# A fused attention and mixture-of-experts block: a shorter gate, own orders for the first and last steps, and the third norm and the logits moved

## The reference

```python
q, k = sigmoid(x @ Wq + bq), sigmoid(x @ Wk + bk);  v = x @ Wv + bv      # 16 heads of 8
sink_in = n / sum(q * cumsum(k));      src_out = n / sum(k * cumsum(q))
cons_sink = sum(q * cumsum(k * src_out)) / n;  cons_src = clip(sum(k * cumsum(q * sink_in)) / n, -1, 1)
v = v * exp(cons_src) / cumsum(exp(cons_src)) * n;   kv = cumsum(k x v)   # outer products, 8x8 a head
h = LN(x + (q * sink_in/n @ kv * sigmoid(cons_sink)) @ Wo + bo)           # first norm
x2 = LN(x + LN(h + gelu(h @ W1 + b1) @ W2 + b2))                          # second and third norm
scores = softmax(x2 @ gate_w + gate_b); top 2 of 8 experts, gate = sum of the two scores
out = LN(x2 + gate * sum over the 2 experts of relu(x2 @ wi + bi + lora_e(x2)) @ wo + bo)   # fourth
```

## Time and profile before

| | |
|---|---|
| median of 3 runs | 451.16 us (450.88 to 452.06) |
| the profiled execution, its own time | 451.44 us |
| its span, first to last instruction | 449.6 us |
| mean granted clock of PE | 0.907 of full |
| busy share PE, DVE, POOL, ACT | 85%, 76%, 50%, 46% |

### The profile page before, as it was taken

The page is one execution under the profiler, slowest core; times in us unless marked ns, Lnnn a source line. Parts: engine busy times, 40 slices in busy tenths (PEclk is TensorE's granted clock), DMA queues, the critical chain, the costliest instruction groups (busy, mean ns, idle before and its releaser), DMA issues.

```text
span 449.6 us, 6354 instructions
## 1 busy us (share of the span) xinstructions
PE 383.4 (85%) x2052; PEld 277.0 (62%) x2052; DVE 341.6 (76%) x819; ACT 208.2 (46%) x375; POOL 226.0 (50%) x263
## 2 busy tenths in 40 slices
PE   4675688488998998899989999899989997897792
PEld 1454556385647873696558665777478756664542
DVE  2448965998799789979897979978997899723522
ACT  2220064247543575446663674167435743554321
POOL 1013633863486349731993359426863498442201
PEclk9556969598999899899998999989998999997897
DMA  8108002700260018000730045002700170000000
GB/s 269 76 7 204 1 0 57 178 2 1 60 176 0 1 27 215 17 1 1 169 89 1 1 111 147 1 1 54 205 1 1 29 183 1 1 24 1 0 23 23
DMA packets 19856, 26.56 MB, mean 59 GB/s; under 512 B 1648, under 2 KB 9968, under 8 KB 19824
## 3 DMA queue, kind: packets, MB, share of 16 engines
q1 hardware_dynamic: 19680, 25.96, 22.6%
q10 hardware_dynamic: 144, 0.21, 0.2%
HBM read 7.29 MB, written 2.10 MB: 21 GB/s over the span
## 4 chain that ended last, share of the span: by engine, by line
PE 38%; DVE 24%; POOL 12%; issue 11%; DMA 7%; ACT 4%; SPq 3%; POOLq 0%; DVEq 0%; ACTq 0%
POOL prod L686 7%; PE pB L332 6%; PE pY L478 5%; DVE kv L870 4%; DMA vb<-vs 4%; PE pY L413 4%; PE pO L386 4%; PE pG L403 4%; DMA xT<-x_t 3%; DVE cum_kv L876 3%; SPq L274 3%; PE pA L320 2%; DVE cum_ks L766 2%; PE pG L467 2%; POOL rstd L676 2%
## 5 line engine op out<-in xcount | busy, mean ns | idle before, releaser
L686 POOL TENSOR_TENSOR prod<-cum_kv,q_fac 128x512 f32<-128x512 f32 x64 | 93.6, 1468 | 24.0 <-DVE cum_kv L876 17.0
L386 PEld LDWEIGHTS pO<-s_wor,prod 128*128 128x128 f32 x512 | 65.8, 200 | 31.7 <-POOL prod L686 22.8
L386 PE MATMUL pO<-s_wor,prod 128*128 128x128 f32 x512 | 70.8, 288 | 15.3 <-POOL prod L686 15.1
L870 DVE TENSOR_TENSOR kv<-k,vb 128x512 f32<-128x512 f32 x64 | 55.3, 864 | 5.5 <-DMA vb<-vs 5.4
L673 POOL TENSOR_TENSOR var_eps<-mv,s_con 128x4 f32<-128x4 f32 x32 | 11.4, 357 | 91.9 <-DVE mv L890 91.9
L876 DVE TENSOR_TENSOR_SCAN cum_kv<-p_ones,cum_kv,kv 128x512 f32<-128x512 f32 x32 | 40.5, 1274 | 0.6
L636 ACT ACTIVATE relu<-pG,s_att 128x512 f32<-128x512 f32 x32 | 21.9, 686 | 38.2 <-PE pG L460 38.0
L478 PEld LDWEIGHTS pY<-s_moe,gel 128*128 128x128 f32 x256 | 36.5, 223 | 4.7 <-issue 4.7
L876 DVE TENSOR_TENSOR_SCAN cum_kv<-p_ones,kv 128x512 f32<-128x512 f32 x32 | 38.5, 1214 | 0.5
L968 DVE SCALAR_TENSOR_TENSOR gel<-pG,neg_bi,relu 128x512 f32<-128x512 f32 x32 | 23.2, 743 | 19.0 <-PE pG L467 19.0
L478 PE MATMUL pY<-s_moe,gel 128*128 128x128 f32 x256 | 37.1, 305 | 0.0
(11 more groups left out here) (135 smaller groups left out, 776.6 us busy)
## 6 DMA issues: line engine op xcount, KB each, us to landing
vb<-vs SPq DMA_DIRECT2D x64, 256.0 KB, 4.6
xT<-x_t SPq DMA_DIRECT2D x8, 256.0 KB, 4.9
xt<-x SPq DMA_DIRECT2D x8, 256.0 KB, 5.3
out<-y SPq DMA_DIRECT2D x8, 256.0 KB, 2.3
s_moe<-moe_w SPq DMA_DIRECT2D x1, 836.0 KB, 10.3
s_wor<-wo_rep SPq DMA_DIRECT2D x1, 512.0 KB, 8.2
s_ffn<-ffn_w SPq DMA_DIRECT2D x1, 512.0 KB, 8.8
s_con<-consts SPq DMA_DIRECT2D x1, 502.0 KB, 5.0
```

The lines of the kernel that those rows point to most:

```text
L386: mm = pe.matmul(pO3[:, s, :], prod[:, m % 4, s * P:(s + 1) * P], s_wor[:, m, :], start=False, stop=(m == DH - 1), skip_group_check=True)
L686: pool.tensor_tensor(prod[:, m % 4, :], cum_kv[t.par][:, m, :], q_fac[t.par][:, :], ALU.mult).then_inc(prod_ready, 1)
L870: dve.tensor_tensor(kv[:, m % 3, :], k[t.par][:, :], vb[:, m, :], ALU.mult).then_inc(kv_ready, 1)
```

## The change

Five edits. (1) The gate has 13 DVE steps instead of 18: the maxima are searched in the logits less their maximum and in their exponentials, not in the normalised scores; the sum of exponentials and its inverse (`sum_exp`, `inverse_sum_exp`) leave the numbered chain, and `gate_total` is `(top2 + 1) * r_ex`. (2) PE, ACT, DVE (and POOL for its second step) get hand-written `opening`, `second_step` and `closing`; steps 1 to 7 still come from `step`, and SP's order is untouched. In the opening PE gets 14 matmuls without use (`keep_busy`), v of tile 0 gets a bank of its own, and ACT runs one sigmoid of one column before the weights are there. In the closing the last tile uses four banks instead of two. (3) In `step`, `moments(c,2)` stands behind the last `outer_product` of the next step, and POOL's `inverse_std(c,2)` behind `product(b,6)`. (4) `x2_T`, `logits` and with them the gate's first steps go behind the first head sums; `expert_out(d,0)` and `(d,1)` go ahead of them. (5) `gate_exp` goes behind `normalise(b,0)` on ACT.

```diff
-GATE_STEPS = 18
+GATE_STEPS = 13
 # PE
+            def opening(a):
+                project_q(a); project_k(a); project_v(a)
+                keep_busy(2)
+                head_sums(a, 0, True); head_sums(a, 0, False)
+                keep_busy(2)
+                denominators_T(a, 0); denominators_T(a, 1)
+                keep_busy(3)
+                head_sums(a, 1, True); head_sums(a, 1, False)
+                keep_busy(1)
+                cumulate_e(a)
+                keep_busy(2)
+                compensation_T(a); factor_T(a)
+                constant_row()
+                project_q(a.plus(1)); project_k(a.plus(1))
+                keep_busy(4)
+                reduce_out(a, 0)
+            def second_step(b):
+                for m in range(1, 5):
+                    reduce_out(b, m)
+                head_sums(a, 0, True); head_sums(a, 0, False); project_v(a)
+                reduce_out(b, 5)
+                denominators_T(a, 0); denominators_T(a, 1)
+                reduce_out(b, 6)
+                head_sums(a, 1, True); head_sums(a, 1, False)
+                reduce_out(b, 7)
+                cumulate_e(a); h_T(b); compensation_T(a); factor_T(a)
+                (hidden, ffn_out, reduce_out(a, 0))
+            def closing(c):
+                inter_base(d, 2); inter1(d, 2); expert_out(d, 0); inter_base(d, 3); inter1(d, 3); expert_out(d, 1)
+                inter2(d, 2); inter2(d, 3); expert_out(d, 2); expert_out(d, 3)
+                x2_T(c); logits(c)
+                inter_base(c, 2); inter_base(c, 3)
+                lora_in(c)
+                inter_base(c, 0); inter_base(c, 1)
+                u_T(c, True); u_T(c, False)
+                (inter1 x4, inter2(0), inter2(1), expert_out and inter2 in turn)
             def step(s):
-                if B: reduce_out(b, 2)
-                if C: x2_T(c)
-                if B: reduce_out(b, 3); reduce_out(b, 4)
-                if C: logits(c)
-                if B: reduce_out(b, 5); reduce_out(b, 6); reduce_out(b, 7)
-                if D: expert_out(d, 0)
+                if B: reduce_out(b, 2); reduce_out(b, 3); reduce_out(b, 4)
+                if D: expert_out(d, 0)
+                if B: reduce_out(b, 5); reduce_out(b, 6); reduce_out(b, 7)
+                if D: expert_out(d, 1)
                 if A: head_sums(a, 0, True); head_sums(a, 0, False); project_v(a)
+                if C: x2_T(c)
+                if D: expert_out(d, 2)
+                if A: denominators_T(a, 0)
+                if C: logits(c)
+                if A: denominators_T(a, 1)
 # ACT
+            act.activation(table_probe[:, :], onesrow[:, 0:1], ACT.Sigmoid)
-                if C: normalise(c, 2); x2T_out(c); gate_exp(c)
-                if A: v_out(a); spread_denominators(a, 0)
+                if C: normalise(c, 2)
+                if A: v_out(a)
+                if C: x2T_out(c)
+                if A: spread_denominators(a, 0); spread_denominators(a, 1)
                 if B: normalise(b, 0)
-                if A: spread_denominators(a, 1)
+                if C: gate_exp(c)
 # POOL
-                if B: product(b, 1); product(b, 2)
+                if B: product(b, 1); product(b, 2); product(b, 3); product(b, 4); product(b, 5); product(b, 6)
                 if C: inverse_std(c, 2)
-                if B: product(b, 3); product(b, 4); product(b, 5); product(b, 6); product(b, 7); inverse_std(b, 0)
+                if B: product(b, 7); inverse_std(b, 0)
 # DVE
                 if B: cumulate_kv(b, 5); outer_product(b, 6); cumulate_kv(b, 6); outer_product(b, 7)
+                if C: moments(c, 2)
                 if B: cumulate_kv(b, 7)
-                if A: cumulate_q(a); cumulate_k(a)
+                if A: cumulate_q(a); cumulate_k(a); k_times_cum_q(a, 0)
                 if D: second_relu(d, 2); second_relu(d, 3)
-                if A: k_times_cum_q(a, 0)
-                if C: gate(c, 0)
                 if A: q_times_cum_k(a, 0)
-                if C: gate(c, 1)
                 if B: moments(b, 0)
-                if C: gate(c, 2)
-                if A: inverse_denominators(a)
-                if C: gate(c, 3)
-                if A: normal_denominators(a)
-                if C: gate(c, 4); gate(c, 5)
-                if C: gate(c, 6); gate(c, 7)
+                if A: inverse_denominators(a); normal_denominators(a)
+                if C: gate(c, 0); gate(c, 1); gate(c, 2); gate(c, 3)
                 if A: sink(a)
                 (from here on one gate call between two calls of tile a, fewer ahead of expert_residual)
-                if B: moments(b, 2)
```

More of the change, by code:

```diff
@@ L56, in wait, with run_steps @@
     eng.wait_ge(sem, value)
-def run_steps(step):
-    for n in range(-1, TILES + 2):
+def run_steps(step, first=-1, end=TILES + 2):
+    for n in range(first, end):
         step(Tile(n))
@@ L534, in step @@
                 if A: factor_T(a)
-                if C: inter1(c, 0); inter1(c, 1); inter2(c, 0); inter2(c, 1)
+                if C: inter_base(c, 0); inter1(c, 0); inter_base(c, 1); inter1(c, 1); inter2(c, 0); inter2(c, 1)
                 if A: reduce_out(a, 0)
-            run_steps(step)
+            opening(Tile(0))
+            second_step(Tile(0))
+            run_steps(step, first=1, end=TILES)
+            closing(Tile(TILES - 1))
         @block.scalar
@@ L740, in _, with second_step @@
             pool.wait_ge(con_loaded, 16)
+            def second_step(b):
+                a = b.plus(1)
+                for m in range(1, DH):
+                    product(b, m)
+                inverse_std(b, 0); e_normal(a); scaled_h(b); h_residual(b); attention_input(a)
+                shifted_x(b); inverse_std(b, 1); product(a, 0); scaled_n2(b)
             def step(s):
@@ L757, in step @@
                 if B: scaled_n2(b)
-            run_steps(step)
+            step(Tile(-1))
+            second_step(Tile(0))
+            run_steps(step, first=1)
         @block.vector
@@ L1020, in step @@
[L1020 to L1021 removed]
                 if A: conserved(a)
[L1023 removed]
+                if C: gate(c, 11)
                 if A: clip_source(a)
@@ L1026, in step @@
                 if A: prefix_e(a)
-                if C: gate(c, 16)
+                if C: gate(c, 12)
                 if A: allocation(a)
-                if C: gate(c, 17); gate_total(c); masked_lora(c, False)
+                if C: gate_total(c); masked_lora(c, False)
                 if A: inverse_cum_e(a); source_factor(a); sink_factor(a)
```

219 lines of the change are left out of this document (155 added, 64 removed).

## The result

The changed kernel takes 459.16 us (median of 4 runs, 456.92 to 462.18) against 451.16: 1.018 times as long, with an interval of 1.012 to 1.024. The forecast was 437 us, faster, with a range of 429 to 446; it is slower, and outside the range. The profiled execution took 457.09 us, with a span of 455.2 us. The four times go with the mean clock granted to PE: 456.92 and 457.09 at 0.917 and 0.914, 461.23 and 462.18 at 0.900. So the profile shows the better of two cases. Among the runs of the experiments one, of gate_only at 453.23 us, counts as slow (more than 1.5% above the fastest of its kernel) and is left out of its median and range.

A forecast was written before the change was run, and what follows sets the result against it. It saw chains binding the opening and end, a loose second stage, and DVE's chain with PE's queue binding full steps; -5.5 - 3.0 + 1.5 + 3.0 + 1.0 - 10.9 = -13.9 from 451.44 gave 437 us, range 429 to 446.

The forecast's parts named there:

- Opening: Start to vs(0): table load and v leave the chain, added matmuls hold PE's clock; -5.5 us, between -3.8 and -6.8.
- The bad end: In the opening: clock falls midway, keep_busy(2) takes 3.4 us instead of 1.7 ahead of compensation_T, costing about 3.
- the part of the clock: In the opening: added matmuls keep PE at full clock, so head sums, transposes and cumulate_e sums run faster; -4.3.
- rival (D): Added matmuls block ready work and the clock drops; opening gives about -1, total 441.5; 0.56 shared with the forecast.
- Second step: vs(0) to vs(1): tile 1's sums interleave with tile 0's, 38.4 instead of 42.3 at full clock; -3.0 us.
- Step 1: Stage of tile 2: POOL's products start late behind inverse_std(b,1), then mostly catch up; +1.5 us (0 to +3).
- Full steps: Steps 2 to 6: net zero at full clock, about +1.2 at half; +0.6 a step, five steps +3.0 us.
- Rival (A): Full steps lose +2 each: idle before the last reduction drops the clock, sink waits for gate; 444 us, chance 0.21.
- Rival (C): Half clock from last reduction to logits in each step, +6 a step, 464 us; decisive above 3.4; chance 0.04.
- rival (B): Full steps gain 0.5 each from shorter gate and earlier head sums, and the ends give all; 429 us, chance 0.17.
- The collision: DVE gate operations slowed beside POOL operations in full steps, 1.21 us instead of 0.18; shift counted in a +0.7.
- Step 7 and closing: After vs(7): step 7 +1.0 from gate_exp's table load and a late last product; closing -10.9 to the end of expert_out.

The follow-up runs named there:

- gate_only: The kernel before with the 13-step gate alone, its steps in the old places; 446.74 us, ratio 0.989.
- late_pool_nokeep: late_pool without the 14 added matmuls of the opening; 439.93 us, ratio 0.975.
- defer_hot: defer with the opening's 14 added matmuls back and two more where PE idled around its head sums; 432.09 us, ratio 0.959.
- late_pool: gate_late with POOL's product(a,0) ahead of inverse_std(b,1) in the second step; 443.25 us, ratio 0.984.
- defer: late_pool_nokeep with POOL's products 1 to 3 of tile 1 moved ahead of norm and residual work in the step after the second; 435.89 us, ratio 0.966.
- gate_late: The changed kernel with DVE's first gate steps moved from ahead of sink to behind cumulate_sink, later ones sliding back; 444.21 us, ratio 0.982.
- pick_late: The changed kernel with only gate steps 3 (pick) and 4 moved behind cumulate_sink; 458.15 us, ratio 1.016.
- fill: The changed kernel with two useless matmuls per step with a tile a, at the second head sums (12 in all); 447.41 us, ratio 0.993.
- ends_only: The changed kernel's opening, second step, closing and short gate, with the old order of step; 440.72 us, ratio 0.974.
- steps_only: The kernel before with the short gate and new order of step on all engines, old opening, second step and closing; 463.38 us, ratio 1.025.
- before_fill: The kernel before with one useless matmul per step ahead of the first head sums; 452.93 us, ratio 1.006.
- second_hot: defer_hot with eight more added matmuls in the second step's PE gaps; 435.83 us, ratio 0.963.

## Why the prediction was wrong

**Opening, -5.5 forecast, -2.4 measured.** The bad end that it named is what came: a fall in the middle and `keep_busy(2)` at half clock, 3.74 us. The profiled runs of the other kernels with this opening show 28.2 to 28.5 us, so -3.5 to -3.8 with nothing changed. But late_pool_nokeep reaches the same 28.39 without the 14 matmuls. So what came is the part of the table load and of v (-2.5 in the forecast, -3.7 measured without the matmuls), and of the part of the clock (-4.3) nothing came. The batches should have ended ahead of PE's next operand; at half clock `keep_busy(2)` stood 1.7 us in front of it, as rival (D) had it. With one matmul more in two places, defer_hot gives -6.1 at clock 1.00, within the range of this term, so the mechanism is sound and the batches were too short.

**Second step, -3.0 forecast, -2.3 measured.** Within its range.

**Step 1, +1.5 forecast, +7.9 measured.** This step failed. The prediction had `product(a,0)` late behind `inverse_std(b,1)`; late_pool took that away and won nothing in the stage. It did not follow what was moved: with the FFN of tile 0 behind `vs`(1), POOL's two residuals come at 81.8 in front of the products. defer shows 2.1 us of it. It also put nothing down for PE, which has 42.95 us of work in this stage instead of 32.78, at a clock of 0.84. And the length of this stage goes with its clock. It takes 56.1 to 57.9 us at 0.74 to 0.78 (gate_late, pick_late, fill, late_pool), 51.7 to 53.3 at 0.82 to 0.84 (late_pool_nokeep, after, ends_only), 49.6 at 0.86 (defer) and 48.9 at 0.89 (defer_hot). Taking the opening's fillers out gave 4.4 us in one pair of kernels, but defer_hot has them all, and two more, and the shortest stage; so they are not the cause as such. What sets the falls there, and the rest to the 46.0 of steps_only, is open. The +7.9 is a mild case, too, since all four kernels of the first group have the opening and the second step of after but for one move on POOL in late_pool.

**Full steps, +0.6 each forecast, +2.2 measured.** This step failed too, and it counts five times. The prediction put `sink` at +10.8 at full clock and +11.8 at half, and called that net zero and +1.2. The place was right (+11.9), and net zero at full clock fits the 47.19 us of steps_only (47.6 on average before); the price of the clock was wrong. It looked for the idle time of PE ahead of the last reduction, and a fall of the clock there. The fall comes at the second head sums: there PE, which was ahead by now, waits 0.66 and 0.89 us for a DVE that had stood 2.90 us at the logits. What is at half clock behind it (`hidden` 2 and 3, `cumulate_e`, the residual's matmul) is the path to `vs`. Undoing the wait (gate_late) and undoing the idle time alone (fill) each bring the clock back to 1.00 in all five stages; these get 17.9 and 13.2 us shorter together, and the kernels 15.0 and 11.8. Rival (A) had the size, +2 a step, and the wait of `sink` for the gate, but the wrong place of the fall. Rival (C) asked for 3.4 us a step and did not come; with step 1's 6.4 us and the opening's 3.1 on top, less was enough to end slower.

**The shorter gate, forecast at nothing.** The prediction held against rival (B) that gate steps 4 to 7 lay in DVE's wait ahead of `q_sink`, so that their removal frees nothing. gate_only takes the gate alone and is 5 us faster, with full stages of 46.0 to 46.4 us. Measured from there, and not from before, the new order of the step cost the changed kernel 17.8 us in its full stages.

**The collision.** `pick` with 1.15 us while `h_res` runs is the hazard that the prediction named from its row. The Trainium skill (GPSIMD Engine Reference, Key points) has VectorE and GpSimd contend for a shared interface; the trace agrees: 1.15 us beside `h_res`, where gate steps of this size take 0.19. At this place it is real and small: with `pick` moved out of the way of `q_sink` (pick_late) the time stayed. At another place it counts, as the last section shows.

**Step 7 and closing, -9.9 forecast, -8.6 measured.** Right, within its range. Logits(7) come 56.95 us behind `vs`(7), against 55.64 before: +1.3 for +1.0. From logits to the end of `expert_out` 18.4 us are left of 28.3: -10.0 for -10.9.

```profile
428.18 1.06 PE L444 MATMUL pM<-s_moe,x2T 128*128 128x8 f32 x8 [0.69 <-ACT x2T L698]
...
444.38 2.16 PE L508 MATMUL pY<-s_moe,gel 128*128 128x128 f32 x16
```

The differences add up: 437.5 + 3.1 + 0.7 + 6.4 + 8.0 + 1.3 = 457.0, against the 457.09 us of the profiled execution.

## What to carry to other kernels

When an operation is put in front of another in an engine's order, ask not only when its operand comes, but what the engine behind does in the meantime: `q_sink` 0.7 us later than before became 2.2 us a step (and 2.5 us later than in gate_late became 3.6), because PE idled in front of short matmuls and then ran the long ones on the path at half clock. Look for the clock where PE waits inside a run of small matmuls, and for what lies behind it; either bring the waiting engine forward, or put a matmul in the gap, sized from the trace, and look at the next gap afterwards, since the fall may only move there. When work of one tile is moved behind a milestone of the next, follow its tail through every engine's order, too: here it came back on POOL one stage later. And take a change apart before you judge it: the part that was priced at nothing, the shorter gate, gave 5 us by itself.

## What the runs showed of the hardware

- In the step shown, one idle of 0.66 and one of 0.89 us around eight short matmuls were followed by some 6.8 us at a granted clock of 0.50 (311.9 to 318.7, if the two mixed windows are split between the two levels). With PE waiting 0 and 0.25 us there (gate_late), or with two matmuls in the gaps (fill), it stayed at 1.00. A fall is likely behind such idles, not certain: with 0.73 and 0.95 us in the first full stage of steps_only it stayed at 1.00, and with 0 and 0.79 us it fell in before_fill (at 256.3) and stayed at 1.00 in three stages of gate_only.
- Added work made the kernel faster: fill has 12 matmuls more than after and is 11.8 us shorter. And added work at half clock costs twice: two fillers take 1.94 us at full and 3.74 at half clock.
- At the same clock of 1.00, full stages of the kernels with the late gate take 46.0 us in one case and 47.1 in another. The traces show what parts them: which operation of DVE meets POOL's `x_bo`. In the first pair of lines, from a stage of 46.0 us of gate_late, `e_pref` starts with it and takes 0.28 us; in the second, from the stage of 47.1, it takes 1.39.

```profile
304.06 1.35 POOL L818 TENSOR_TENSOR x_bo<-xt,s_row 128x512 f32<-128x512 f32 x1
304.08 0.28 DVE L989 TENSOR_TENSOR_SCAN e_pref<-s_con,esrc 128x64 f32<-128x64 f32 x1
...
349.86 1.26 POOL L818 TENSOR_TENSOR x_bo<-xt,s_row 128x512 f32<-128x512 f32 x1
349.88 1.39 DVE L989 TENSOR_TENSOR_SCAN e_pref<-s_con,esrc 128x64 f32<-128x64 f32 x1
```

PE's `cumulate_e` waits for `e_pref`, so those 1.1 us lie on the path to `vs`. In the first case `delta`, off the path, is held instead (1.19 us). All 30 full stages of gate_late, late_pool, late_pool_nokeep, defer, defer_hot and second_hot go with it: the 18 with an `e_pref` of 0.28 us take 46.0 to 46.5 us, the 12 with 1.39 or 1.40 take 47.1 to 47.9. What decides which of the two is held was not tested. late_pool has four such stages, late_pool_nokeep three, defer two, defer_hot one: much of the 1.4 us that defer won in steps it doesn't touch.
